# An attention kernel whose context sums move into its first phase and whose 64-key attentions run one unit deeper

## The reference

```
L0: q from x (64 rows a batch), k and v from [ctx; x] (128 rows), 16 heads of 64
    scores = ((q + content_bias) k^T + rel_shift((q + position_bias) (pe Wr)^T)) * scale
    x = LN(x + softmax(scores) v Wo);  x = LN(x + relu(x W1 + b1) W2 + b2)
L1: x = LN(x + att(x, x));  x = LN(x + att(x, ctx))     16 heads of 8, 64 keys, masked
    x = LN(x + relu(x W1 + b1) W2 + b2)
L2: pooled = mean(ctx, tokens of a batch);  x = LN(x + gate(x, pooled) * proj(pooled))
L3: x = x + att(LN(x), LN(x));  x = x + att(LN(x), LN(ctx))   16 heads of 8, 64 keys
    x = x + sum over the top 2 of 8 experts of gate * fc2(gelu(fc1(LN(x))))
```

## Time and profile before

| | |
|---|---|
| median of 3 runs | 2027.27 us (2026.01 to 2027.56) |
| the profiled execution | 2030.62 us, of it the span of its instructions 2029.1 us |
| busy share of the span | TensorE 82%, its weight loads 64%, VectorE 68%, ScalarE 56%, GpSimd 47% |
| mean granted TensorE clock | 0.915 of full speed |
| first attention | to about 634 us; a tile in (581.6-99.3)/27 = 17.86 us |
| feed-forward 0; attentions 0 and 1 | to 713 us; to 1120 us |
| feed-forward 1; L2; attentions 2 and 3 | to 1205 us; to 1310 us; to about 1700 us |
| routing; experts | to 1800 us; to the end |

### The profile page before, as it was taken

How to read it: one execution, slowest core, us unless ns; L and a number is a source line. 1 busy time by engine, 2 the same in 40 slices (tenths; PEclk the granted TensorE clock), 3 DMA queues, 4 the chain that set the end, 5 groups by cost and what they waited for, 6 DMA issues and landing times. The chain is left out here.

```text
span 2029.1 us, 56439 instructions
## 1 busy us (share of the span) xinstructions
PE 1658.9 (82%) x17626; PEld 1291.2 (64%) x17626; DVE 1376.8 (68%) x4296; ACT 1144.0 (56%) x3299; POOL 959.4 (47%) x1434
## 2 busy tenths in 40 slices
PE   5899999999996879998888765369998885439882
PEld 5788888888884756666666652146666664337771
DVE  2677777777776568787777547867787774328773
ACT  1577777777773345666665322247777773117771
POOL 1434444443433434556666423434444443646773
PEclk9999999999998989999999785779999996559996
DMA  6766666666660032220000000000000000126665
GB/s 184 147 152 151 151 145 143 157 144 150 151 149 25 0 133 96 94 81 16 16 16 13 1 0 1 0 4 0 0 6 11 12 12 11 46 96 199 211 209 157
DMA packets 214507, 166.84 MB, mean 82 GB/s; under 512 B 27344, under 2 KB 188496, under 8 KB 214160
## 3 DMA queue, kind: packets, MB, share of 16 engines
q1 hardware_dynamic: 205840, 142.85, 28.3%
q0 software_dynamic: 8576, 22.88, 3.3%
HBM read 91.92 MB, written 73.76 MB: 82 GB/s over the span
## 5 line engine op out<-in xcount | busy, mean ns | idle before, releaser
L842 POOL TENSOR_TENSOR sb_work<-sb_work,sb_cols 128x512 f32<-128x512 f32 x128 | 134.4, 1050 | 299.2 <-ACT sb_work L1056 191.0
L701 ACT ACTIVATE sb_probs<-sb_probs,sb_work 128x128 f32<-128x128 f32 x512 | 198.7, 407 | 114.4 <-DVE sb_work L626 114.4
L983 DVE TENSOR_REDUCE sb_work<-PS 128x8 f32<-128x512 f32 x256 | 175.1, 684 | 53.1 <-PE PS L883 53.0
L280 POOL TENSOR_SCALAR sb_next_var_eps<-sb_next_moments 128x1 f32<-128x1 f32 (+1 forms) x184 | 43.4, 236 | 321.5 <-DVE sb_next_moments L275 321.3
L1021 ACT ACTIVATE sb_work<-sb_work 128x512 f32<-128x512 f32 x256 | 161.2, 630 | 56.0 <-DVE sb_work L985 55.8
L861 PE MATMUL PS<-sb_ident,sb_work 128*128 128x128 f32 x1024 | 165.2, 285 | 33.6 <-ACT sb_work L1021 28.2
L985 DVE TENSOR_TENSOR sb_work<-PS,sb_work 128x512 f32<-128x512 f32 x256 | 176.9, 691 | 8.8
L861 PEld LDWEIGHTS PS<-sb_ident,sb_work 128*128 128x128 f32 x1024 | 114.7, 143 | 68.5 <-ACT sb_work L1021 55.2
L906 PE MATMUL PS<-sb_v_ones,sb_work 128*64 128x18 f32 x4096 | 144.7, 214 | 1.9 <-ACT sb_work L1027 1.8
L906 PEld LDWEIGHTS PS<-sb_v_ones,sb_work 128*64 128x64 f32 x4096 | 132.2, 139 | 19.6 <-issue 7.3
L1027 ACT ACTIVATE sb_work<-PS 128x512 f32<-128x512 f32 x256 | 139.4, 595 | 4.9 <-PE PS L861 1.7
(11 more groups left out here) (273 smaller groups left out, 4472.7 us busy)
## 6 DMA issues: line engine op xcount, KB each, us to landing
rel_scratch<-sb_work SPq DMA_DIRECT2D x64, 516.0 KB, 7.7
sb_work<-rel_scratch SPq DMA_DIRECT2D x64, 512.0 KB, 6.6
expert_rows<-sb_blank SPq DMA_DIRECT2D x36, 520.0 KB, 2.9
sb_w_up<-expert_halves SPq DMA_DIRECT2D x23, 512.0 KB
sb_w_down<-expert_halves SPq DMA_DIRECT2D x23, 512.0 KB
expert_halves<-sb_e_halves POOLq DMA_DIRECT2D x16, 512.0 KB, 5.8
sb_work<-expert_rows SPq DMA_DIRECT2D x23, 260.0 KB, 3.5
sb_e_raw<-e_W POOLq DMA_DIRECT2D x16, 256.0 KB, 6.8
```

Of the source, the lines that this page charges most:

```text
L701: ins = e.activation(probs[:, j], probs[:, j], ACT.Exp, bias=neg_max[:, j:j + 1], scale=-1.0, accum_out=row_sum[:, j:j + 1])
L842: e.tensor_tensor(k_masked[:, u], k_sb[:, u].rearrange("p (b k) -> p b k", b=2).unsqueeze(2) .to_broadcast([P, 2, 4, S]), col("place").uns ...
L983: e.tensor_reduce(top, mine, AX.X, ALU.max).then_inc(sem("att_max_ready"), 1)
```

## The change

**One unit deeper, four steps a pass.** `walk_pair` gives the head to tile n+3 and the front to tile n+2; the back and late roles stay. The loops are unrolled by four. `att_probs` and `v_ones` have four buffers instead of two; the semaphores' counts move by one.

```diff
     def roles(n):
-        return [pair[t // units] if 0 <= t < 2 * units else None for t in (n + 2, n + 1, n, n - 1)]
+        return [pair[t // units] if 0 <= t < 2 * units else None for t in (n + 3, n + 2, n, n - 1)]
     def alone(n):
-        step(n // 2, n % 2, *roles(n))
-
-    for n in range(-2, 2):
+        step(n // 4, n % 4, *roles(n))
+
+    for n in range(-3, 4):
         alone(n)
-    with e.Fori(1, units // 2 - 1) as k:
-        for u in range(2):
-            step(k, u, *roles(2))
-    for n in range(units - 2, units + 2):
+    with e.Fori(1, units // 4 - 1) as k:
+        for u in range(4):
+            step(k, u, *roles(4))
+    for n in range(units - 4, units + 4):
         alone(n)
-    with e.Fori(units // 2 + 1, units - 1) as k:
-        for u in range(2):
-            step(k, u, *roles(units + 2))
-    for n in range(2 * units - 2, 2 * units + 1):
+    with e.Fori(units // 4 + 1, units // 2 - 1) as k:
+        for u in range(4):
+            step(k, u, *roles(units + 4))
+    for n in range(2 * units - 4, 2 * units + 1):
         alone(n)
```

```diff
-        l0_loads = {"rel": [(wr, a["l0_Wr"]), (peT, a["peT"]), (content_bias[:, :], a["l0_cb"]),
+        l0_loads = {"rel": [(ident[:, :], a["ident"]), (wr, a["l0_Wr"]), (peT, a["peT"]), (content_bias[:, :], a["l0_cb"]),
...
                 load_tokens(t, t)
             for dst, src in loads:
                 e.dma_start(dst, src).then_inc(sem("params_loaded"), 16)
-            e.wait_ge(sem("params_loaded"), 16 * len(loads))
-            meet(e, 0)
...
         def l0_pool(e, c):
             e.memset(half_power[:, :], -0.5)
             e.memset(zeros[:, :], 0.0)
...
+            e.wait_ge(sem("l0_table_drained"), 6)
+
+            def prepare_later():
+                e.wait_ge(sem("params_loaded"), 16 * len(loads))
+                e.tensor_copy(ident_16[:, :], ident[:, :])
+                e.tensor_copy(bv_wide[:, 0], col("sa_bv").to_broadcast([P, P]))
+                e.tensor_copy(bv_wide[:, 1], col("ca_bv").to_broadcast([P, P])).then_inc(sem("bases"), 1)
+                e.tensor_tensor(bases[:, 0], row("ln11_b"), row("ca1_bo"), ALU.add)
+                e.memset(blank[:, :, 0:D], 0.0)
+                e.memset(blank[:, :, D + 1:ROW], 0.0)
+                e.tensor_copy(blank[:, :, D:D + 1].bitcast(U32), ids[:, 2 * NT:].unsqueeze(2)).then_inc(sem("blank_ready"), 1)
...
+                if isinstance(n, int) and n == 2:
+                    prepare_later()
...
+                if has(3):
+                    t = n + 3
+                    wait_alone(e, sem("ctx_moments"), t + 1)
+                    e.tensor_tensor(c_moments[:, :, bass.ds(t, 1)].rearrange("p b a m -> p b (a m)"), c_last,
+                                    zeros[0:S, 0:1].unsqueeze(2).to_broadcast([S, 2, 2]), ALU.add)\
+                        .then_inc(sem("ctx_moments_kept"), 1)
+                if has(0):
-            e.wait_ge(sem("l0_vo_loaded"), 32)
-            for g in range(4):
-                o = bank()
-                for i in range(4):
-                    h = head_at(4 * g + i)
-                    ins = e.matmul(o[:, i * P:(i + 1) * P], wvT[:, h], wo0[:, h], start=True, stop=True)
-                ins.then_inc(sem("l0_table_done"), 1)
-            e.wait_ge(sem("bases"), 1)
-            for i, n in enumerate(("sa", "ca")):
-                ins = e.matmul(PS[:, 2, P * i:P * i + P], bv_wide[:, i], w_out[n][:, :], start=True, stop=True)
-            ins.then_inc(sem("bases"), 1)
-            meet(e, 0)
+            e.wait_ge(sem("l0_qk_loaded"), 32)
+            e.wait_ge(sem("l0_table_drained"), 6)
...
+                if isinstance(n, int) and n == -3:
+                    e.wait_ge(sem("l0_vo_loaded"), 32)
+                    for g in range(4):
+                        e.wait_ge(sem("l0_rel_kept"), g + 1)
+                        for i in range(4):
+                            h = head_at(4 * g + i)
+                            ins = e.matmul(PS[:, 4 + g, i * P:(i + 1) * P], wvT[:, h], wo0[:, h], start=True, stop=True)
+                        ins.then_inc(sem("l0_table_done"), 1)
             walk_ahead(e, NT, step)
+            e.wait_ge(sem("bases"), 1)
+            for i, n in enumerate(("sa", "ca")):
+                ins = e.matmul(PS[:, 2, P * i:P * i + P], bv_wide[:, i], w_out[n][:, :], start=True, stop=True)
+            ins.then_inc(sem("bases"), 1)
...
-                    e.wait_ge(sem("l0_table_done"), n + 1)
-                    e.tensor_copy(to[:, 4 * g:4 * g + 4], PS[:, n % 2].rearrange("p (i k) -> p i k", i=4))\
-                        .then_inc(sem("l0_table_drained"), 1)
-                    n += 1
-            e.wait_ge(sem("bases"), 2)
-            for i, bias in enumerate(("sa_bo", "ca_bo")):
-                e.tensor_tensor(bases[:, 1 + i], PS[:, 2, P * i:P * i + P], row(bias), ALU.add)
-            meet(e, 0)
+            e.tensor_tensor(w_k0_lo[:, :], w_k0, w_k0_hi[:, :].bitcast(F32), ALU.subtract)\
+                .then_inc(sem("l0_setup_kept"), 1)
...
+                    e.tensor_reduce(pooled[:, bass.ds(2 * t, 2)],
+                                    transposed.rearrange("p (b a k) -> p a b k", b=2, a=2)[:, 0], AX.X, ALU.add)
...
                 if has(0):
+                    if isinstance(n, int) and n == 0:
+                        e.wait_ge(sem("params_loaded"), 16 * len(loads))
                     e.wait_ge(sem("l0_out_done"), n + 1)
...
+                if isinstance(n, int) and n == -3:
+                    for g in range(4):
+                        e.wait_ge(sem("l0_table_done"), 6 + g + 1)
+                        e.tensor_copy(VO[:, 4 * g:4 * g + 4], PS[:, 4 + g].rearrange("p (i k) -> p i k", i=4))\
+                            .then_inc(sem("l0_table_drained"), 1)
                 if has(1):
                     normalise(3)
+                if has(3):
+                    t = n + 3
+                    wait_alone(e, sem("ctx_moments_kept"), t)
+                    for b in range(2):
+                        ins = e.bn_stats(c_stats[:, b], kv_in[0:S, (u + 3) % 4, b])
+                    ins.then_inc(sem("ctx_stats"), 1)
+                    wait_alone(e, sem("ctx_stats"), t + 1)
+                    for b in range(2):
+                        ins = e.bn_aggr(c_last[:, b], c_stats[:, b])
+                    ins.then_inc(sem("ctx_moments"), 1)
```

```diff
-                        wait_alone(e, sem("ctx_moments"), m - 1)
...
+            if c["i"] == 0:
+                e.wait_ge(sem("ctx_moments_kept"), NT + 1)
+                for b in range(2):
+                    e.dma_start(ctx_norm[S * b:S * b + S], c_norms[:, :, b]).then_inc(sem("ctx_spread"), 16)
...
+            if base == 0:
+                e.wait_ge(sem("ctx_moments_kept"), NT)
+                e.tensor_scalar(c_var_eps, c_moments[:, :, :, 1], EPS, None, ALU.add).then_inc(sem("ctx_var_eps"), 1)
+                e.tensor_tensor(c_norms[:, 0], c_moments[:, :, :, 0], zeros[0:S, 0:1].unsqueeze(2).to_broadcast([S, 2, NT]), ALU.add)
+                e.wait_ge(sem("ctx_var_eps"), 1)
+                e.tensor_tensor(c_norms[:, 1], c_var_eps, half_power[0:S, 0:1].unsqueeze(2).to_broadcast([S, 2, NT]), ALU.pow)\
+                    .then_inc(sem("ctx_moments_kept"), 1)
...
-                if front and front["cross"] == 0:
-                    t = n + 1 - front["i"] * NT
-                    inv_std_pool(e, "ctx", t + 1, c_moments, c_var_eps, ctx_mean, ctx_inv_std, t, 1)
...
-                n = base + 2 * k + u
+                n = base + 4 * k + u
+                u3, w3 = (u + 3) % 2, (u + 3) % 4
                 if back:
                     transpose_probs(n, u, 0)
                     wait(e, sem("att_ctx_ready"), n)
                     transpose_probs(n, u, 1)
                 if front:
-                    c, m, v = front, n + 1, 1 - u
+                    c, m, v = front, n + 2, u % 2
                     e.wait_ge(sem("att_k_masked"), m + 1)
                     wait(e, sem("att_shifted"), 2 * m)
                     if c["mask"]:
...
-                    e.wait_ge(sem("att_normed"), n + 3)
-                    wait(e, sem("att_T_kept"), n + 2)
+                    e.wait_ge(sem("att_normed"), n + 4)
+                    wait(e, sem("att_T_kept"), n + 3)
...
-                    e.matmul(PS[:, 7, 0:P], wq, yT[:, u], start=True, stop=True)
-                    e.matmul(PS[:, 7, P:2 * P], wk, src[:, u], start=True, stop=True)
+                    e.matmul(PS[:, 7, 0:P], wq, yT[:, u3, :, 0], start=True, stop=True)
+                    e.matmul(PS[:, 7, P:2 * P], wk, src[:, u3, :, 0], start=True, stop=True)
                     for b in range(2):
-                        for half in range(2):
-                            ins = e.matmul(PS[S * half:S * half + S, 7, (2 + b) * P:(3 + b) * P],
-                                           src[:, u, S * b:S * b + S], wv, start=True, stop=True)
```

(39 more changed lines are left out.)

129 lines of the change are left out of this document (63 added, 66 removed).

## The result

The changed kernel takes 2036.20 us (median of 6 runs, 2030.63 to 2039.27), the kernel before 2026.64 us beside it (6 runs). The ratio is 1.0043, 95% interval 1.0028 to 1.0058: slower by 0.4%, where 1999 us was forecast. The profiled execution's span is 2034.5 us, 5.4 us over the 2029.1 us before.

The account below looks back on a forecast made before the run. TensorE was taken to bound the first attention, a ring through several engines the 64-key attentions. Setup -16, context sums +17, attentions -35, power +4, depth +2 sum to -28 us: 2027.3 to 1999 us, range 1985 to 2013.

Parts of the forecast that it names:

- The step that failed: First attention: the context's statistics, aggregations and sum on VectorE make tiles 0.6 us later, +17 us over 29 tiles.
- The "slower" one: First attention: VectorE overruns 1.5 us a tile and TensorE's clock drops, +69 instead of +17, 2051 us; chance 0.08.
- The stretch itself: First attention: VectorE's gapless work until `x_lo` ends, with 0.45 us slack; tiles forecast at 18.3 to 18.6 us.
- the overlap of independent statistics: First attention, VectorE: back-to-back statistics overlap by 0.08-0.1 us, four in 0.87 us; without overlap about 28 us, not 17.
- Setup: Before the first tile: parameter loads no longer waited for, second tile's kept scores earlier, -16 us (bounds 10 and 18.4).
- Attentions: 64-key attentions: dropped context sums, V projection without tiling switch and fewer branches shorten tiles, -35 us in all.
- Depth: 64-key attentions: transposes stop waiting for exponentials, but masked keys stay one step ahead of scores; worth nothing by itself.
- the fill and drain: Attention pairs: a deeper start adds about 4.7 us, the drain returns 3.6; +1 a pair, +2 us.
- The power: Start of attention 0: GpSimd raises 64 columns to a power in 10 to 12 us, 4 us left over.

Follow-up runs that it names:

- the padded kernel: The changed kernel with 70 one-column memsets ahead of VectorE's setup, so its first-attention loop starts 70 instructions later: 2002.47 us, ratio 0.9853 to the kernel before.

## Why the prediction was wrong

**The step that failed** is the first attention's. It set 0.95 us of added work against a slack of 0.45 us ("Together 0.95, over the slack by 0.5 us") and so counted instructions only by their durations; the room that their code takes was a term put at nothing, without a reason. 29 x 0.6 = 17 us was forecast; 47.8 came, of which 36.9 us are the fetched code (five stalls of 6.8 to 7.5 us, with the clock's dips behind them) and 10.9 us the stretch. No rival named it. The "slower" one put its price on VectorE's work and decided from tiles of 19.6 us; the mean was 19.6, by another mechanism.

**The stretch itself** was right in kind and somewhat large: tiles of 18.3 us padded, as forecast, `x_lo` late by 23.3 us in 24 cases, 0.40 us a tile rather than 0.6 and 10.9 us in all rather than 17. The prediction held the overlap of independent statistics against the Trainium skill's page on VectorE. The same section of the Trainium skill (VectorE: DVE Perf Modes, The DRAIN you can't avoid) adds that a next operation that isn't held starts earlier, so the 0.87 us for four do not contradict it.

**Setup**: -16 forecast, -16.2 in the changed kernel, -16.5 alone. The transposes began at 19.2 and the second tile's kept scores at 42.1 us, both as written (timeline of the changed kernel):

```profile
19.21 0.66 PE L527 MATMUL PS<-sb_ident,sb_kv_in 128*128 128x128 f32 x2 [3.84 <-DMA mask<-mask]
...
42.10 2.48 DVE L651 TENSOR_TENSOR sb_work<-PS,sb_work 128x512 f32<-128x512 f32 x4 [5.50 <-DMA rel_scratch<-sb_work]
```

**Attentions**: -35 forecast for the tiles. In the changed kernel the masked keys give, with the ends, (943.7-757.8)/32 = 5.81, 5.60, 5.26 and 5.50 us, against 5.67, 5.8, 5.2 and 5.65 forecast. In the padded kernel, counted by the first masked keys of each attention and the last of each pair, the four attentions are 5.1, 20.3, 3.0 and 10.0 us shorter than before, 38 us in all, where 9.5, 15, 4.5 and 5.5 were forecast. So the whole was right and its parts were not; that the misses cancelled is luck. Attention 0 keeps a slow tile behind the branch: its passes go 5.80, 5.52, 6.41 and 5.52 us, not three times 5.58 and once 5.93. In attention 3 some 5 us can be had without this change (last section).

```profile
L883 POOL TENSOR_TENSOR sb_work<-sb_work,sb_cols x33: 1046/1048/1049, 757.8 to 943.7; 128x512 f32<-128x512 f32 x33
...
L883 POOL TENSOR_TENSOR sb_work<-sb_work,sb_cols x31: 1046/1047/1051, 949.1 to 1117.1; 128x512 f32<-128x512 f32 x31
...
L883 POOL TENSOR_TENSOR sb_work<-sb_work,sb_cols x33: 1046/1047/1050, 1350.3 to 1518.5; 128x512 f32<-128x512 f32 x33
...
L883 POOL TENSOR_TENSOR sb_work<-sb_work,sb_cols x30: 1046/1047/1049, 1528.9 to 1688.4; 128x512 f32<-128x512 f32 x30
```

**Depth**: worth nothing to a tile, as written. The transposes did stop waiting for the exponentials (55.2 us of it before; in the changed kernel most of what is left is "issue"), and the tile did not follow:

```profile
L899 PEld LDWEIGHTS PS<-sb_ident,sb_work 128*128 128x128 f32 x1024 | 117.4, 145 | 45.9 <-issue 30.4
```

But the fill and drain were put at +2 us and cost 11. That "the drain returns 3.6" had no row behind it, and the drain did not return it.

**The power**: 10.54 us and 4 us left over (first masked keys 12.3 us behind the phase's start instead of 8.3), both as forecast.

```profile
746.22 10.54 POOL L858 TENSOR_TENSOR sb_c_norms<-sb_c_var_eps,sb_half_power 64x64 f32<-64x64 f32 x1
```

With the fetch taken away the forecast stands: 0.9853 of 2027 us is 1997 us (1993 to 2002), and 1999 was predicted. That sum held partly by luck, since +9 us of depth stood against -3 us in the attentions and -6 us in the stretch.

## What to carry to other kernels

Before instructions are added to a loop, count how many the fullest engine issues in one pass, and where the loop begins; here a loop that reached over a fourth block of code lost 36.9 us, more than the 10.9 us that the added work cost, and code added ahead of the loop did the same. A wait put down to "issue" for microseconds, once a pass and on one engine, with packets on the instruction queue, was the sign of it. A deeper pipeline pays only if the link that sets the period runs through the place that was deepened; here it did not, and one more step to fill and drain cost 4.0 and 7.0 us in the two pairs.

## What the hardware showed beyond that

A smaller effect of the same kind stands in the attentions, whose loops are short. In the kernel before, VectorE's idle time at the branch of attention 3 is 0.75 us; with the same code at another place (the kernel without the sums of attention 1) it is 0.65. Timelines, one row of each:

```profile
1559.91 0.35 DVE L962 TENSOR_SCALAR sb_work<-sb_work,sb_ctx_mean,sb_ctx_inv_std 128x128 f32<-128x128 f32 x1 [0.75 <-issue]
```

```profile
1551.23 0.35 DVE L961 TENSOR_SCALAR sb_work<-sb_work,sb_ctx_mean,sb_ctx_inv_std 128x128 f32<-128x128 f32 x1 [0.65 <-issue]
```

Tiles there alternate 5.50 and 6.07 us in the first and 5.50 and 5.85 us in the second. With one tile of 7.8 us that only the first has, this is 5 us over the attention. The kernel before with 64 memsets shows the faster pattern in attention 3 too, and in attention 0 the slower one: 0.60 us of idle time at the branch where the kernel before has 0.50, and 6.33 us for the tile behind it instead of 6.22.

```profile
831.09 0.35 DVE L971 SCALAR_TENSOR_TENSOR sb_work<-sb_X,sb_tile_mean,sb_rows 128x128 f32<-128x128 f32 x1 [0.60 <-issue]
```

A block boundary inside the loop would explain all of it. Counted as above, the slow loops hold the instructions 1932 to 1989 (attention 3 before) and 1066 to 1125 (attention 0 with 64 memsets), the fast ones 1901 to 1958 (attention 3 without the sums of attention 1), 1996 to 2053 (attention 3 with 64 memsets) and 1002 to 1061 (attention 0 before). With a boundary at one place in every 128, from the 43rd to the 68th, the first two cross it, the other three do not, and the first attention's loops still fit. That is read from where they lie; no run was made for it.
